# First token group's softmax and norms in halves of two tiles on three engines, second products of tiles 5 to 7 later, and unread matmuls in the waits

## The chip, the cores and the metric

One Trainium2 chip, one core of it. The metric is the device time of one execution of the whole kernel in microseconds; less is better. The kernel before took 384.93 us (median of 3 runs, 383.13 to 386.03).

## The reference, cut to what matters

Four blocks work on x of 4 x 256 tokens with 256 features. The first attention block fills most of the kernel and is the same in both kernels. The other three are where the change lies:

```python
def fp8_matmul(x2d, w):
    x8 = (x2d / scale_x).astype(float8_e4m3fn)
    w8 = (w / scale_w).astype(float8_e4m3fn)
    return (x8 @ w8.T) * (scale_x * scale_w)

x = x + L0_xattn(layernorm(x), ctx, ...)                        # x1
h = square(relu(fp8_matmul(layernorm(x), w_fc)))                # "expand"
x = x + fp8_matmul(h, w_proj)                                   # x2; "contract", the second products
scores = (qp @ kp.T) / 8 * layernorm(x)                         # qp, kp from ctx; gated by the normed x
x = x + softmax(where(mask, -inf, scores))                      # x3
y = layernorm(x)
h1 = rmsnorm(y, norm1_w);  h = y + (h1 @ wv + bv) @ wo          # "attend"
h2 = rmsnorm(h, norm2_w)
mlp = (silu(h2 @ w_gate) * (h2 @ w_up)) @ w_down                # 256 -> 704 -> 256
x = x + where(sigmoid(y @ w_router + b_router) > 0.5, h + mlp, y)
```

## The kernel before, in words

The 1024 tokens are 8 tiles of 128 rows (`NT`); a tile is one 128 x 256 slice of `xs` (the running x) and `xn` (its normed or gated form). Two groups of four tiles, 0 to 3 and 4 to 7, go one after the other through everything behind the expanding product. The matmuls of the last block run on 512 tokens, one group, at a time.

Each engine has its instruction list written out by hand, in the order in which it is issued; an engine works through its list in order, and a wait on a semaphore holds all that stands behind it. There is no planner: `@block.tensor`, `@block.vector`, `@block.scalar`, `@block.gpsimd` and `@block.sync` are the five lists, and semaphores (`x2_ready`, `norm_ready`, ...) tie them together. SyncE's list has only loads of weights, long done here, and the eight stores at the end.

For a group the steps are, with their engine and line:

- VectorE rounds `relu` (the squared activations) to two fp8 parts for each tile: `h8_halved(t)` (L1264) and `h8_shared(t)` (L1271). ScalarE turns the halved part into its form for the product, `rounded_top(t)` (L776). TensorE's `contract(t)` (L1832) multiplies both parts, 16 matmuls, and `x2_tile(t)` (L1183) on VectorE adds the result to `xs` and takes statistics.
- `aggregate` and `newton` give the inverse standard deviation. Its first guess is a power on GpSimd (`powers`, L535). Small steps that need each other have a semaphore wait between them (`in_order`).
- `gate_scores`, `mask_scores`, `largest` (L1195 to L1212) on VectorE make the masked scores of four tiles and their row maxima; `softmax(c)` (L791) on ScalarE is four Exp with row sums; `x3_sums` and `x3_statistics` (L1214, L1223) add the softmax to `xs` and take the statistics of the sum.
- `norm_rows(c)` (L802) on ScalarE normalises the four tiles. `turn_norm(c)` (L1843) on TensorE transposes them, `turned_copy` (L567) on ScalarE copies that to `tailT`, `attend(c)` (L1846) multiplies it with the folded value and output weights: 16 matmuls of 256 columns. GpSimd's `shifted_tiles` (L540) adds the bias row to the normed tiles.
- `h_tile(t)` (L1242) on VectorE makes h, `h_square_sum(t)` (L820) on ScalarE its sum of squares, `h_square` (L1249) and `newton` the scale, `h2_tiles` (L1255) the scaled rows. TensorE transposes them (`turn(2, atbuf, ...)`, L1872), `tail_copy` (L808) on ScalarE and `tail_lows` (L1316) on VectorE split them into a high and a low part.
- `gate_high(n)` and `gate_low(n)` (L1881, L1893) are gate and up for the n-th block of 128 of the 704 features. `silus(n)` (L830), `gated(n)` (L1333), `high_part(n)` (L837) and `low_part(n)` (L1340) make the activations, `down` (L1901) the last product.

In the order before, TensorE does the products of tiles 4 and 5 in one go ahead of the first group's transposes, and those of 6 and 7 right behind `attend(0)`. The second group's softmax chain starts when `x2_tile(7)` is done, so it lies beside the gate and up products of the first group. The Exp of all four tiles of the second group stand ahead of the first `silus`.

`keep_busy(n, spare, w)` (L1741) issues n bf16 matmuls of w columns (512 unless given) into a PSUM bank that nobody reads: they compute nothing of the result.

Of the kernel before, what the change touches and what calls it, by code (L numbers as in the profile page):

```python
# [23 lines left out]
P = 128  # L24
# [81 lines left out]
def build(nc, x, ctx_t, ctx_n, blob, const_a, const_b, wq1_t, wk1_t, attn_mask, key_mask,  # L106
          w_fc_t, w_proj_t, small, w_router, wv_t, wo, w_gate, w_up, w_down, out):
    with ExitStack() as ctx:
# [3 lines left out]
        def sem(name):  # L112
            return ctx.enter_context(nc.semaphore(name))
# [192 lines left out]
        v_first, shift3_ready = sem("v_first"), sem("shift3_ready")  # L306
        gated_high, gated_low = sem("gated_high"), sem("gated_low")
# [27 lines left out]
        def rots(n):  # L335

            return rot_low[n % 2][:], rot_up[:], rot_z[n % 2][:]

# [94 lines left out]
        def _(pool):  # L433
# [106 lines left out]
            def shifted_tiles(gr):  # L540

                pool.wait_ge(vo_copied, 3)
                for t in range(gr * NT // 2, (gr + 1) * NT // 2):
                    pool.wait_ge(norm_ready, NT + t + 1)
                    pool.tensor_tensor(atbuf(t), xn[:, t, :], bvo, ALU.add).then_inc(shifted_ready, 1)
# [12 lines left out]
            pool.wait_ge(norm_ready, 2 * NT)  # L558
# [7 lines left out]
        def _(act):  # L566
# [224 lines left out]
            def softmax(c):  # L791
                act.wait_ge(gated_ready, c + 1)
                for t in range(4 * c, 4 * c + 4):
                    act.activation(xn[:, t, :], xn[:, t, :], ACT.Exp, bias=c_m[:, t:t + 1],
                                   accum_out=ssq[:, t:t + 1]).then_inc(soft_ready, 1)
# [3 lines left out]
            softmax(0)  # L799
            rounded_top(5)  # L800

            def norm_rows(c):  # L802
                act.wait_ge(shift3_ready, c + 1)
                for t in range(4 * c, 4 * c + 4):
                    act.activation(xn[:, t, :], xs[:, t, :], ACT.Identity, bias=negmean[:, t:t + 1],
                                   scale=rstd[:, t:t + 1]).then_inc(norm_ready, 1)
# [11 lines left out]
            rounded_top(7)  # L818

            def h_square_sum(t):  # L820

                act.wait_ge(h_ready, t + 1)
                act.activation(mbias[:, t, :], hbuf(t), ACT.Square, accum_out=ssq[:, t:t + 1]).then_inc(ssq_ready, 1)

            for t in range(4):
                h_square_sum(t)
            tail_copy(0)
            softmax(1)
# [16 lines left out]
            silus(0)  # L845
            silus(1)
# [32 lines left out]
        def _(dve):  # L879
# [321 lines left out]
            def mask_scores(gr):  # L1201
                lo, hi = groups[gr]
                newton(4 + 4 * gr, rstd, lo, hi)
# [6 lines left out]
            def largest(gr):  # L1210
                lo, hi = groups[gr]
                dve.tensor_reduce(c_m[:, lo:hi], xn[:, lo:hi, :], AX, ALU.max, negate=True).then_inc(gated_ready, 1)  # L1212

            def x3_sums(gr):  # L1214

                lo, hi = groups[gr]
# [5 lines left out]

            def x3_statistics(gr):  # L1223

                lo, hi = groups[gr]
# [3 lines left out]
                in_order(ins)  # L1229
                aggregate(5 + 4 * gr, lo, hi)  # L1230
# [3 lines left out]

            def norm_tiles(gr):

                lo, hi = groups[gr]
                newton(5 + 4 * gr, rstd, lo, hi)
                for t in range(lo, hi):
                    normalise(t).then_inc(norm_ready, 1)  # L1240
# [36 lines left out]
            for t in range(3):  # L1277
# [12 lines left out]
            gate_scores(0)  # L1290
            mask_scores(0)
            largest(0)
            h8_shared(4)
            h8_halved(5)
            h8_shared(5)
            x3_sums(0)
            x3_statistics(0)
            x2_tile(4)
            newton(5, rstd, 0, half)
            dve.scalar_tensor_tensor(out=negmean[:, 0:half], in0=mv[:, 0:half, 0], scalar=-1.0, in1=rstd[:, 0:half],  # L1300
                                     op0=ALU.mult, op1=ALU.mult).then_inc(shift3_ready, 1)
            h8_halved(6)
            h8_shared(6)
            x2_tile(5)
            dve.wait_ge(variance_ready, 6)
            newton(6, r1, 0, half, of=(c_q, c_y1))
            h8_halved(7)
            h8_shared(7)
            for t in range(half):
                h_tile(t)  # L1310
            h_square(0)
            x2_tile(6)
            dve.wait_ge(variance_ready, 7)
            newton(7, r2, 0, half)
            h2_tiles(0)
            def tail_lows(c):  # L1316
# [6 lines left out]

            in_order(x2_tile(7))
# [3 lines left out]
            mask_scores(1)  # L1328
            largest(1)
            tail_lows(0)  # L1330
            x3_sums(1)

# [42 lines left out]
            x3_statistics(1)  # L1375
# [54 lines left out]
        def _(pe):  # L1430
# [412 lines left out]
            def turn_norm(c):  # L1843
                turn(1, lambda t: xn[:, t, :], norm_ready, NT, (2 * c, 2 * c + 1))
# [15 lines left out]
            keep_busy(18, 1)  # L1860
            contract(4)
            contract(5)
            keep_busy(16, 1)
            pe.wait_ge(qk_copied, 8)
            turn_norm(0)
            attend(0)
            contract(6)
            contract(7)

            pe.wait_ge(wgu_low, 4)  # L1870
            keep_busy(10, 4)
# [47 lines left out]
            pe.wait_ge(h_ready, 4)  # L1919
            pe.wait_ge(x2_ready, NT)  # L1920
            for n in range(3):
                gate_high(n)
# [102 lines left out]
```

## Time and profile before

| | before |
|---|---|
| median of 3 runs | 384.93 us (383.13 to 386.03) |
| the profiled execution's time | 386.52 us |
| its span, first to last instruction | 384.4 us |
| mean granted TensorE clock | 0.991 |
| TensorE busy | 366.5 us (95%) |
| VectorE busy | 295.8 us (77%) |
| ScalarE busy | 208.5 us (54%) |
| GpSimd busy | 174.5 us (45%) |

The span is what the trace covers; the profiled execution's time holds 2.1 us more around it. The granted clock is the share of full TensorE speed that the chip granted (1.00 is 2.4 GHz, 0.50 is 1.2 GHz). Busy shares are means over stages with different limits. The changed part begins near 294 us and ends near 346 us; all ahead of it is the same in both kernels, and all behind it is the same work in the same order. A start time in the rows below is counted from the first instruction; "idle before" with a releaser names what the engine waited for.

### The profile page before, as it was taken

Reading aid. Unit: us, or ns where it says so; the run is one execution under the profiler, and the core shown is the slowest. Engines: PE = TensorE matmul, PEld = TensorE weight load, DVE = VectorE, ACT = ScalarE, POOL = GpSimd, SP = SyncE. Lnnn points to the kernel's source line nnn. Section 1 sums busy time; section 2 is a strip of 40 time slices with the busy share of each in tenths; the row PEclk is TensorE's granted clock in tenths of the full one; section 3 lists DMA queues with packets and bytes.
Section 4 is the critical chain, followed back from the end, with each engine's and each line's share of the span. In section 5 each row is a group of like instructions: output and inputs, shape, how many; then the busy total and the mean of one; then the engine's idle time right before and its main releaser. Section 6 shows DMA issues by size and latency. Waiting matters only on the chain.

```text
span 384.4 us, 6374 instructions
## 1 busy us (share of the span) xinstructions
PE 366.5 (95%) x2185; PEld 267.3 (70%) x2185; DVE 295.8 (77%) x674; ACT 208.5 (54%) x555; POOL 174.5 (45%) x163
## 2 busy tenths in 40 slices
PE   8799999999999999999999999998999789989996
PEld 8775676677676766776767677764556467879885
DVE  5698698698667886976697765578899967897773
ACT  1524476457546664765576494617974362582240
POOL 2454665476448645764665430671801232056100
PEclk9999999999999999999999999999999969999999
DMA  7639100300301103000004000400000000000001
GB/s 245 213 112 342 62 1 0 111 3 1 112 0 46 65 0 112 3 0 2 0 3 150 3 0 2 119 0 3 0 3 0 0 2 0 3 0 2 28 28 56
DMA packets 9087, 17.55 MB, mean 46 GB/s; under 512 B 2144, under 2 KB 6944, under 8 KB 8160
## 3 DMA queue, kind: packets, MB, share of 16 engines
q1 hardware_dynamic: 9056, 17.14, 13.3%
q8 instruction: 18, 0.29, 0.3%
q14 instruction: 13, 0.11, 0.1%
HBM read 16.09 MB, written 1.05 MB: 45 GB/s over the span
## 4 chain that ended last, share of the span: by engine, by line
PE 67%; DVE 14%; ACT 7%; POOL 6%; issue 3%; DMA 2%; SPq 0%; DVEq 0%; POOLq 0%
PE bank L1524 16%; PE bank L1595 7%; PE bank L1570 7%; PE bank L1586 6%; PE bank L1554 4%; PE bank L1539 3%; PE bank L1476 3%; PE bank L1616 2%; PE bank L1839 2%; DVE relu L1159 2%; PE bank L1443 2%; DMA blobs<-in_blob 2%; POOL prob L463 2%; PE bank L1851 2%; PE bank L1445 1%
## 5 line engine op out<-in xcount | busy, mean ns | idle before, releaser
L463 POOL TENSOR_TENSOR prob<-prob,rinv 128x512 f32<-128x512 f32 x64 | 65.9, 1041 | 74.4 <-DVE rinv L1023 74.4
L1524 PE MATMUL bank<-xnT,w 128*128 128x512 f32 x288 | 90.2, 434 | 1.7 <-DVE xnT L920 1.7
L621 ACT ACTIVATE prob<-bank,negmax 128x256 f32<-128x256 f32 x128 | 59.0, 478 | 29.5 <-DVE negmax L1017 29.5
L1017 DVE TENSOR_REDUCE negmax<-bank 128x2 f32<-128x512 f32 x64 | 40.8, 680 | 35.3 <-PE bank L1570 35.3
L1524 PEld LDWEIGHTS bank<-xnT,w 128*128 128x128 f32 x288 | 50.4, 189 | 19.5 <-issue 13.3
L631 ACT COPY probT<-bank 128x512 f32<-128x512 f32 x64 | 37.7, 589 | 22.8 <-PE bank L1586 22.8
L951 DVE TENSOR_TENSOR rot_up<-bank,cb 64x512 f32<-64x512 f32 x64 | 44.1, 689 | 1.6
L458 POOL TENSOR_TENSOR rot_low<-rot_low,rot_up 128x512 f32<-128x512 f32 x32 | 41.0, 1281 | 3.8 <-DVE rot_up L951 3.8
L1586 PE MATMUL bank<-ca,prob 128*128 128x128 f32 x256 | 39.4, 276 | 0.5 <-ACT probT L631 0.3
L1586 PEld LDWEIGHTS bank<-ca,prob 128*128 128x128 f32 x256 | 29.1, 140 | 13.8 <-issue 5.3
L443 POOL TENSOR_TENSOR c_y<-c_ve,minus_half 128x4 f32<-128x4 f32 (+1 forms) x9 | 9.8, 1086 | 61.2 <-DVE c_ve L901 45.5
L1570 PEld LDWEIGHTS bank<-ktmp,uT 64*128 64x128 f32 x256 | 23.4, 186 | 13.4 <-issue 11.3
L1570 PE MATMUL bank<-ktmp,uT 64*128 64x256 f32 x256 | 32.0, 389 | 0.0
L456 POOL TENSOR_TENSOR rot_z<-rot_z 128x512 f32<-128x512 f32 x16 | 21.1, 1322 | 23.8 <-DVE rot_z L951 23.8
L1595 PE MATMUL bank<-probT,kva 128*64 128x256 f32 x256 | 31.1, 384 | 0.5
L1616 PE MATMUL bank<-wkvo,cT 128*128 128x256 f32 x128 | 29.7, 381 | 0.0
L621 ACT ACTIVATION_READ_ACCUMULATOR prob<-bank,negmax 128x1 f32 x128 | 26.7, 209 | 0.0
L1595 PEld LDWEIGHTS bank<-probT,kva 128*64 128x64 f32 x256 | 17.7, 137 | 12.7 <-ACT probT L631 3.9
L1616 PEld LDWEIGHTS bank<-wkvo,cT 128*128 128x128 f32 x128 | 23.5, 190 | 3.9 <-issue 1.2
L946 DVE TENSOR_TENSOR rot_low<-bank,cb 128x512 f32<-128x512 f32 x32 | 21.9, 685 | 4.6 <-PE bank L1524 4.6
L636 ACT COPY cT<-bank 128x512 f32<-128x512 f32 x15 | 8.8, 585 | 28.4 <-PE bank L1595 28.4
L951 DVE TENSOR_TENSOR rot_z<-bank,cb 64x512 f32<-64x512 f32 x32 | 22.0, 688 | 0.4
(212 smaller groups left out, 706.8 us busy)
## 6 DMA issues: line engine op xcount, KB each, us to landing
blobs<-in_blob SPq DMA_DIRECT2D x7, 1024.0 KB, 4.9
xs<-in_x SPq DMA_DIRECT2D x2, 512.0 KB, 4.1
xn<-in_w_fc_t SPq DMA_DIRECT2D x1, 1024.0 KB, 4.9
ctxT<-in_w_proj_t SPq DMA_DIRECT2D x1, 1024.0 KB, 5.3
out<-qk SPq DMA_DIRECT2D x8, 128.0 KB, 1.7
cb<-in_const_b SPq DMA_DIRECT2D x1, 768.0 KB, 9.0
blobs<-in_w_gate SPq DMA_DIRECT2D x1, 704.0 KB, 5.2
blobs<-in_w_up SPq DMA_DIRECT2D x1, 704.0 KB, 6.5
```

Of the source, the lines that this page charges most:

```text
L458: pool.tensor_tensor(low[:, r, :], low[:, r, :], up[:, r, :], ALU.add).then_inc(joined, 1)
L463: pool.tensor_tensor(p[:], p[:], rinv[:, n % PROBS, :].unsqueeze(2).to_broadcast([P, 2, S]), ALU.mult).then_inc(normed, 1)
L621: ins = act.activation(prob[n % PROBS][:, st, :], pS[n % UNITS][:, st * S:(st + 1) * S], ACT.Exp, bias=negmax[:, n % UNITS, st:st + 1], ac ...
L631: act.copy(probT[n % UNITS][:].rearrange("p a s -> p (a s)"), pT[:]).then_inc(probsT_copied, 1)
L946: dve.tensor_tensor(tokens(rope_parts(m)[0]), tokens(src[:]), angles(cosq, r), ALU.mult)
L951: ins = dve.tensor_tensor(tokens(crossed[to:to + DC, :]), tokens(src[lo:lo + DC, :]), angles(sinq, r, lo, lo + DC), ALU.mult)
L1017: dve.tensor_reduce(negmax[:, n % UNITS, :], pS[n % UNITS][:].rearrange("p (a s) -> p a s", a=2), AX, ALU.max, negate=True).then_inc(max_r ...
L1524: ins = pe.matmul(q_bank(m)[:], w[a][:, k, r * P:(r + 1) * P], x[b][:, k, c * CH:(c + 1) * CH], start=(i == 0), stop=(i == 5))
L1570: ins = pe.matmul(pS[2 * a + h][:, st * S:(st + 1) * S], uT[g % 2][lo:hi, at:at + P], ktmp[lo:hi, b * S:(b + 1) * S], start=True, stop=True)
L1586: ins = pe.transpose(pT[:, lt * S + st * P:lt * S + (st + 1) * P], prob[n % PROBS][:, st, lt * P:(lt + 1) * P], ident)
L1595: ins = pe.matmul(o[h * DC:(h + 1) * DC, :], kva[:, 2 * b + lt, :], probT[2 * a + h][:, lt, :], start=(lt == 0), stop=(lt == 1))
L1616: return pe.matmul(bank[OUT_BANK[t // 2]][:, t % 2 * D:(t % 2 + 1) * D], cT[:, f, t * P:(t + 1) * P], wkvo[:, f, :], start=(f == 0 and t % ...
```

## The change

It moves and splits work; no product, softmax or norm is dropped. `normalise(t)` is an existing helper (L904), one VectorE `tensor_scalar` for a tile.

1. The first group's (and the second's) `mask_scores`, `largest`, `softmax` and `x3_sums` now take two tiles at a time, `two` = 0 to 3. The statistics stand in `x3_sums`; `x3_squares` holds what is left of `x3_statistics`.
2. In the first group tiles 0 and 1 are normalised on VectorE, tiles 2 and 3 on ScalarE; a new semaphore `first_normed` counts the former, and `norm_of(t)` says what to wait for.
3. The h8 roundings of tiles 5 to 7 and `x2_tile` of 4 to 6 stand at other places of VectorE's list, `rounded_top(7)` behind `h_square_sum`.
4. TensorE: `contract(5)` behind `attend(0)`, `contract(7)` behind `gate_high(0)`. Unread matmuls: 25 for 18, 19 for 16 at another place, 4 new ones ahead of `attend(0)`, and 10 taken out ahead of the transposes of h2.
5. ScalarE runs `softmax(2)`, `silus(0)`, `softmax(3)`, `silus(1)`, where it ran one softmax of four tiles ahead of the first `silus`.

The diff, cut to its core:

```diff
+        def norm_of(t):
+            return (first_normed, t + 1) if t < 2 else (norm_ready, NT + t - 1)
...
 # GpSimd: shifted_tiles
-                    pool.wait_ge(norm_ready, NT + t + 1)
+                    pool.wait_ge(*norm_of(t))
...
 # ScalarE
-            def softmax(c):
-                act.wait_ge(gated_ready, c + 1)
-                for t in range(4 * c, 4 * c + 4):
+            def softmax(two):
+                act.wait_ge(gated_ready, two + 1)
+                for t in range(2 * two, 2 * two + 2):
...
             softmax(0)
+            softmax(1)
             rounded_top(5)
             def norm_rows(c):
                 act.wait_ge(shift3_ready, c + 1)
-                for t in range(4 * c, 4 * c + 4):
+                for t in range(2 if c == 0 else 4, 4 * c + 4):
...
             norm_rows(0)
             turned_copy(4, tailT, turned_copied, (0, 1))
             rounded_top(6)
-            rounded_top(7)
             for t in range(4):
                 h_square_sum(t)
+            rounded_top(7)
             tail_copy(0)
-            softmax(1)
+            softmax(2)
...
             silus(0)
+            softmax(3)
             silus(1)
...
 # VectorE
             gate_scores(0)
+            newton(4, rstd, 0, half)
             mask_scores(0)
             largest(0)
+            mask_scores(1)
+            largest(1)
             h8_shared(4)
+            x3_sums(0)
+            in_order(x3_sums(1))
+            aggregate(5, 0, half)
             h8_halved(5)
-            h8_shared(5)
-            x3_sums(0)
-            x3_statistics(0)
-            x2_tile(4)
             newton(5, rstd, 0, half)
             dve.scalar_tensor_tensor(out=negmean[:, 0:half], ...).then_inc(shift3_ready, 1)
+            for t in range(2):
+                normalise(t).then_inc(first_normed, 1)
+            x3_squares(0)
+            h8_shared(5)
             h8_halved(6)
-            h8_shared(6)
-            x2_tile(5)
             dve.wait_ge(variance_ready, 6)
             newton(6, r1, 0, half, of=(c_q, c_y1))
+            h_tile(0)
+            x2_tile(4)
+            h_tile(1)
+            h_tile(2)
+            h_tile(3)
+            h8_shared(6)
+            h_square(0)
             h8_halved(7)
             h8_shared(7)
-            for t in range(half):
-                h_tile(t)
-            h_square(0)
-            x2_tile(6)
             dve.wait_ge(variance_ready, 7)
             newton(7, r2, 0, half)
             h2_tiles(0)
+            x2_tile(5)
...
+            tail_lows(0)
+            x2_tile(6)
             in_order(x2_tile(7))
             aggregate(8, half, NT)
             dve.wait_ge(qk_copied, 8)
             gate_scores(1)
-            mask_scores(1)
-            largest(1)
-            tail_lows(0)
-            x3_sums(1)
+            newton(8, rstd, half, NT)
+            mask_scores(2)
+            largest(2)
+            mask_scores(3)
+            largest(3)
+            x3_sums(2)
...
             gated(0)
-            x3_statistics(1)
+            in_order(x3_sums(3))
+            aggregate(9, half, NT)
+            x3_squares(1)
             gated(1)
...
 # TensorE
             pe.wait_ge(x2_ready, 3)
-            keep_busy(18, 1)
+            keep_busy(25, 1)
             contract(4)
-            contract(5)
-            keep_busy(16, 1)
+            keep_busy(19, 1)
             pe.wait_ge(qk_copied, 8)
             turn_norm(0)
+            keep_busy(4, 1)
             attend(0)
+            contract(5)
             contract(6)
-            contract(7)
             pe.wait_ge(wgu_low, 4)
-            keep_busy(10, 4)
             turn(2, atbuf, h2_ready, 0, (0, 1))
...
             pe.wait_ge(h_ready, 4)
+            gate_high(0)
+            contract(7)
+            gate_high(1)
             pe.wait_ge(x2_ready, NT)
-            for n in range(3):
-                gate_high(n)
+            gate_high(2)
             for n in range(3):
                 gate_low(n)
```

## Rows read from the trace of the kernel before

**Rows 1.** Timeline of TensorE, first group: start us, length us, work, idle before.
```profile
300.08 3.65 PE L1839 MATMUL bank<-wpr,tail_all 128*128 128x256 bf16 x32 [1.66 <-DVE tail_all L1273]
303.57 3.62 PE L1743 MATMUL bank<-wfc,ident 128*128 128x512 bf16 x16
308.13 0.73 PE L1438 MATMUL bank<-ca,xn 128*128 128x128 f32 x2 [0.94 <-ACT xn L805]
...
311.00 6.78 PE L1851 MATMUL bank<-cb,tailT 128*128 128x256 f32 x16 [0.72 <-ACT tailT L571]
317.62 3.66 PE L1839 MATMUL bank<-wpr,tail_all 128*128 128x256 bf16 x32
...
324.74 0.47 PE L1890 MATMUL bank<-tail_hi,wgu_high 128*128 128x512 f32 x1 [0.43 <-ACT tail_hi L812]
```

**Rows 2.** Windows view: stretch, length, busy of each engine, granted clock, DMA.
```profile
310.40:311.00 0.60, 0.00 (x0) 0.00 (x0) 0.56 (x2) 0.60 (x3) 0.60 (x2) 0.50 0.00 0
```

**Rows 3.** The timeline of TensorE, second group.
```profile
339.87 1.03 PE L1438 MATMUL bank<-ca,xn 128*128 128x128 f32 x8
341.72 3.69 PE L1851 MATMUL bank<-cb,tailT 128*128 128x256 f32 x16 [0.82 <-ACT tailT L571]
345.60 0.39 PE L1443 MATMUL bank<-wd_high,gated_hi 128*128 128x256 f32 x1 [0.18 <-DVE h_rows L1246]
```

**Rows 4.** The timeline of VectorE from 298 us on.
```profile
298.06 1.22 DVE L1212 TENSOR_REDUCE c_m<-xn 128x4 f32<-128x1024 f32 x1
299.19 0.74 DVE L1273 TENSOR_SCALAR tail_all<-relu,sc 128x1024 fp8e4<-128x1024 f32 x1
...
301.63 1.67 DVE L1220 SCALAR_TENSOR_TENSOR xs<-xn,c_r,xs 128x256 f32<-128x256 f32 x4
...
305.07 0.17 DVE L901 TENSOR_SCALAR c_ve<-mv 128x4 f32<-128x4 f32 x1
...
309.45 0.52 DVE L891 SCALAR_TENSOR_TENSOR c_t<-c_y 128x4 f32<-128x4 f32 x1
...
317.82 0.48 DVE L1246 SCALAR_TENSOR_TENSOR h_rows<-bank,r,at_rows 128x256 f32<-128x256 f32 x1 [0.80 <-PE bank L1851]
318.88 0.17 DVE L1252 TENSOR_SCALAR c_ve<-ssq 128x4 f32<-128x4 f32 x1 [0.58 <-ACT mbias L823]
...
321.00 1.14 DVE L1260 TENSOR_SCALAR at_rows<-h_rows,r 128x256 f32<-128x256 f32 x4
322.06 0.48 DVE L1186 SCALAR_TENSOR_TENSOR xs<-bank,sc,xs 128x256 f32<-128x256 f32 x1
...
335.99 0.68 DVE L1337 TENSOR_TENSOR tail_all<-bank,tail_all 128x512 f32<-128x512 f32 x1
...
338.22 1.29 DVE L1337 TENSOR_TENSOR tail_all<-bank,tail_all 128x512 f32<-128x512 f32 x2
```

**Rows 5.** The timeline of ScalarE.
```profile
301.30 1.04 ACT L779 ACTIVATE tail_all<-prob 128x1024 bf16<-128x1024 fp8e4 x1
307.38 2.08 ACT L805 ACTIVATE xn<-xs,negmean,rstd 128x256 f32<-128x256 f32 x4 [5.05 <-DVE negmean L1300]
...
323.91 1.26 ACT L812 ACTIVATE tail_hi<-bank,sm 128x512 fp32r<-128x512 f32 x2 [5.06 <-PE bank L1438]
...
330.31 0.50 ACT L794 ACTIVATE xn<-xn,c_m 128x256 f32<-128x256 f32 x1
...
330.92 1.28 ACT L835 ACT_TABLE_LOAD   x1
332.21 1.09 ACT L835 ACTIVATE tail_all<-bank 128x512 f32<-128x512 f32 x2
```

**Rows 6.** The page's costliest groups: a reduction of 512 columns.
```profile
L1017 DVE TENSOR_REDUCE negmax<-bank 128x2 f32<-128x512 f32 x64 | 40.8, 680 | 35.3 <-PE bank L1570 35.3
```

**Rows 7.** The timeline of GpSimd.
```profile
308.12 3.18 POOL L545 TENSOR_TENSOR at_rows<-xn,cb 128x256 f32<-128x256 f32 x4 [0.82 <-ACT xn L805]
...
336.52 1.01 POOL L443 TENSOR_TENSOR c_y<-c_q,minus_half 128x4 f32<-128x4 f32 x1
```

More of the change, by code:

```diff
@@ L306, in build @@
         v_first, shift3_ready = sem("v_first"), sem("shift3_ready")
+        first_normed = sem("first_normed")
         gated_high, gated_low = sem("gated_high"), sem("gated_low")
@@ L556, in _ @@
             powers(11, 1, c_ve, c_y)
-            pool.wait_ge(norm_ready, 2 * NT)
+            pool.wait_ge(*norm_of(NT - 1))
             pool.wait_ge(h2_ready, NT)
@@ L1199, in gate_scores, with mask_scores @@
                                              op0=ALU.subtract, op1=ALU.mult).then_inc(gate_done, 1)
-            def mask_scores(gr):
-                lo, hi = groups[gr]
-                newton(4 + 4 * gr, rstd, lo, hi)
+            def mask_scores(two):
+                lo, hi = 2 * two, 2 * two + 2
                 dve.wait_ge(gate_done, hi)
@@ L1208, in mask_scores, with largest, x3_sums @@
                 in_order(ins)
-            def largest(gr):
-                lo, hi = groups[gr]
+            def largest(two):
+                lo, hi = 2 * two, 2 * two + 2
                 dve.tensor_reduce(c_m[:, lo:hi], xn[:, lo:hi, :], AX, ALU.max, negate=True).then_inc(gated_ready, 1)
-            def x3_sums(gr):
-                lo, hi = groups[gr]
+            def x3_sums(two):
+                lo, hi = 2 * two, 2 * two + 2
                 dve.wait_ge(soft_ready, hi)
@@ L1221, in x3_sums @@
                                              in1=xs[:, t, :], op0=ALU.mult, op1=ALU.add).then_inc(x3_ready, 1)
-            def x3_statistics(gr):
-                lo, hi = groups[gr]
                 for t in range(lo, hi):
@@ L1228, in x3_statistics, with x3_squares @@
                     ins = dve.bn_stats(stats[:, t, :], xs[:, t, :])
-                in_order(ins)
-                aggregate(5 + 4 * gr, lo, hi)
+                return ins
+            def x3_squares(gr):
+                lo, hi = groups[gr]
                 in_order(dve.reciprocal(c_q[:, lo:hi], c_ve[:, lo:hi]))
@@ L1233, in x3_statistics @@
                 dve.tensor_scalar(c_q[:, lo:hi], c_q[:, lo:hi], 1e-6, None, ALU.add).then_inc(variance_ready, 1)
[L1235 to L1240, printed above, removed]
             def h_tile(t):
@@ L1843, in turn_norm @@
             def turn_norm(c):
-                turn(1, lambda t: xn[:, t, :], norm_ready, NT, (2 * c, 2 * c + 1))
+                for k in range(DK):
+                    for t in range(4):
+                        if k == 0:
+                            pe.wait_ge(*norm_of(4 * c + t))
+                        ins = pe.transpose(bank[4 + 2 * c + k][:, t * P:(t + 1) * P],
+                                           xn[:, 4 * c + t, k * P:(k + 1) * P], ident)
+                    ins.then_inc(turned, 1)
             def attend(c):
```

## The prediction

> **What bounds the kernel now.** I read the granted clock first, then TensorE's rows in time order, then the chain of waits and the rows of VectorE, ScalarE and GpSimd around it. TensorE is busy 95% of the span, so I looked for where its start times come from. Between the products of tile 3 and `gate_high(0)` (L1921) it mostly runs matmuls that nobody reads. It waits for `h8_shared(4)`, then for the normalised rows; transposes run from 308.13 us, `attend(0)` from 311.00 [rows 1]. The granted clock is 0.50 there, the 1.2 GHz level [rows 2]. The 16 matmuls of `attend(0)` take 6.78 us; the same 16 in `attend(1)` take 3.69 at the full clock [rows 1, 3]. So the profiled execution holds a clock loss of 3.09 us in front of everything later. Its time was 386.52 us (span 384.4 and 2.1 around it); without that loss it would be 383.4, near the lowest of the three runs, 383.13. The median, 384.93, lies 1.6 below the profiled execution, and I take the spread for that loss in different lengths.
>
> From 324.74 to 339.87 TensorE runs 66 matmuls of gate and up without a gap, 0.229 us each [rows 1, 3]: `gate_high` (8 of them) is 1.83, `gate_low` (4) 0.92. What sets the end lies beside it: `x2_tile(7)` at 322.06, statistics, gating, softmax of tiles 4 to 7, the Silu table at 330.92, `gated`, `norm_rows(1)`, `gated(2)` at 338.22, and the products `down_two(0)` at 345.60, released by VectorE's `h_tile(5)` [rows 3, 4, 5]. The reader is to see two queues with nearly the same end: TensorE is free for transposes at 339.87, and the last rows they need come at 339.8. So the change pays only as far as it moves `x2_tile(7)` and `gated(2)`.
>
> **The change, first group.** (a) *Softmax in halves.* The reduction of 1024 columns takes 1.22 us; for 512 I take 0.69, between half of it (0.61) and the 0.68 of a 128x512 reduction elsewhere [rows 4, 6]. Two reductions and one more wait put the last maximum at 299.51 instead of 299.28, but ScalarE has tiles 0 and 1 done by 299.1 and starts the last two at 299.54. A tile costs it 0.50 [rows 5], so the exponentials end at 300.6 (301.4 before). VectorE has `h8_shared(4)` done at 300.17 (0.66 a step, 0.74 long) [rows 4] and goes straight into the sums: `h8_halved(5)` and `h8_shared(5)`, 1.32 us, no longer stand ahead. Sums, statistics and aggregates of four tiles took 3.44 (301.63 to 305.07) [rows 4]; with one more reciprocal, 0.2, `c_ve` starts at 304.01, 1.06 earlier.
>
> (b) *Norms on three engines.* The power on GpSimd takes 1.01 [rows 7] and ends at 305.27; `h8_halved(5)` (to 304.94) lies beside it, and `rounded_top(5)`, 1.04 on ScalarE [rows 5], ends at 306.03, just ahead of `norm_rows`. The Newton steps and the shift end at 306.04. VectorE normalises tiles 0 and 1 (0.28 a step, as `h2_tiles`) [rows 4], ScalarE tiles 2 and 3 at 0.52 each [rows 5]: last row at 307.16, before 309.46. The transposes, copies and `attend` followed the last row by 1.54 (309.46 to 311.00), so `attend(0)` starts at 308.7, 2.3 earlier. The unread matmuls cost nothing while they end inside waits: 0.217 each [rows 1], 25 of them end at 299.8 before `contract(4)` (300.25 to 302.0), 19 end at 306.15, and the 4 behind the transposes 0.1 before `attend`. If they overran, the bounds are nothing and 0.9 us, all four. I take nothing. With them no stretch without matmuls is longer than 0.4 us, so I expect 3.7 us for `attend(0)`: end 312.4.
>
> (c) *h and h2.* `x3_squares(0)`, after the two norms, gives GpSimd its second power until 308.2; `shifted_tiles(0)` runs to 311.4. `newton(6)` lies beside it and was slow there, 1.9 us (309.45 to 311.33, first step 0.52) [rows 4]; bounds 0.6 and 1.9, and I take 1.9: VectorE is free for `h_tile(0)` at 310.3. `x2_tile(4)` (0.9) goes behind it; `h_tile(3)` waits for `attend`: 312.5, before 317.82. The row sum, power, Newton steps and `h2_tiles` take 1.06, 1.25, 0.7 and 1.14 [rows 4, 7]: h2 is ready at 316.67; `h8_shared(6)`, `h8_halved(7)` and `h8_shared(7)` fit into the waits, `rounded_top(7)` (314.4 to 315.5) too. ScalarE copies 0.45 after the last row, and `gate_high(0)` follows the copy's start by 0.83 (323.91 to 324.74) [rows 1, 5]: 317.95, 6.8 earlier than before.
>
> (d) *Later products.* A `contract` is 1.75 (two took 3.66) [rows 1]. 5 and 6 run 312.45 to 315.95, beside the wait for h2, at no cost; were that cover gone they would cost 3.5. `contract(7)` comes behind `gate_high(0)`: 319.8 to 321.55, and `x2_tile(7)` at 321.7. **Before it was 322.06, so of 6.8 us only 0.36 reach the second group.** `x2_tile(5)`, the two `tail_lows` and `x2_tile(6)` end at 320.0, so none delays it.
>
> **The change, second group.** From `x2_tile(7)` to the maxima as before, minus 0.36; halves give the first maximum at 327.11, the last at 328.65. ScalarE now runs `softmax(2)`, `silus(0)`, `softmax(3)`, `silus(1)`. Before, the only table load between Exp and Silu took 1.28, from 330.92, and Silu began at its end, 332.21 [rows 5]. With Exp again behind Silu there are three loads instead of one, 2.57 us more. Exp ends for tiles 4 and 5 at 328.15; load, `silus(0)` to 330.05; load to 331.34; Exp of tiles 6 and 7 to 332.35 (all four before: 330.9); load, `silus(1)` to 334.25. VectorE has the sums of tiles 4 and 5 done and `gated(0)` at 330.93. Behind 332.38 stand 0.21 + 0.84 + 0.7 for tiles 6 and 7, aggregates 0.6: `c_ve` done at 334.74, GpSimd's two powers to 336.85, Newton steps 0.6, `gated(2)` at 337.45, before 338.22. **Gain 0.77**: halving saves more on this chain than the two loads take. What is queued behind is `norm_rows(1)`, 337.05 instead of 337.72, then the same copies, `low_part`s beside GpSimd's shifts, `h_tile(5)`, and `down_two(0)` at 344.8 for 345.60. `gate_high(4)` waits for `gated(0)` (331.0) and `gate_high(5)` for `gated(1)`, at 335.99 before and 335.95 now [rows 4]: TensorE stands idle from 333.7 to 336.0, time it had won. From 345.60 on both kernels do the same work, so the 0.77 stays.
>
> The Trainium skill, "ScalarE: Activation LUTs", section "What ACT_TABLE_LOAD costs", gives about 1.28 us for the load and about 1.38 more for a drain at every switch; its section "Table sets: the hidden batching unit" asks for all calls of one set together, which speaks against this order. By its price, two switches instead of none before the last Exp would give 388.5 us by my estimate. The row here has no drain behind the load.
>
> Sum: 386.52 - 0.77 = **385.7 us**, 0.8 above the median of the runs before, 0.8 below the profiled one, and 2.3 above 383.4, what the old order takes when its clock holds. It is no measurable change. Within 1% means 381.1 to 388.8; less than 1% is about what a measurement of this kernel can't tell from nothing.
>
> **The rivals.** *The clock falls in the second wait (slower).* Place: TensorE between 333.7 and 340.65. In it lie 2.3 us idle, six matmuls (1.4 us), 0.8 idle, eight transposes, 0.75 idle; before the loss at 310.4 stood 3.8 us with only eight transposes [rows 1, 2]. It decides if the clock is down when `attend(1)` starts at 340.65: at 6.78 it would end at 347.4, and `down_two(0)` waits for it and not for `h_tile(5)`: 2.6 us later, 388.3, slower than before by 1.8 against the profiled execution and 3.4 against the median; with the products behind it slow too, up to 390. Against: the idle 1.66 us before 300.08 [rows 1] and the 0.82 before `attend(1)` [rows 3] did not lower it, and the six matmuls break the stretch. 0.22. *A switch costs more than its row*, or the first half's close fits (`rounded_top(5)`, the 4 unread matmuls) fail: each 0.1 to 2.7, to 388.4. 0.06. *Silu and Exp share one table.* Then Exp of tiles 6 and 7 ends at 331.0 and `gated(2)` comes at 336.1: 384.4. Against: a load stands between Exp and Silu now. 0.06. *TensorE is the bound after all*: the six gate steps, 15.13, and `contract(7)` from 317.95 end at 334.9, 4.9 before 339.87: 381.6, down to 380 if the second group follows. It needs my chain from `x2_tile(7)` to `gated(2)` to be 4 us too long, though it is made of rows. 0.10.
>
> **How the numbers follow.** Forecast 0.56, with its own range of 384.2 to 387.2: newton(6) at 0.6 takes nothing off, since `h_tile(3)` waits for TensorE; a reduction of 0.61 takes 0.3 off; the run-to-run spread is 383.1 to 386.0. The range 382.8 to 388.3 leaves out most of the last rival and the upper half of the first. Faster by over 1%: 0.6 of the last rival and a tail of the forecast, 0.10. Slower by over 1%: the first rival's upper part, 0.09, and the second's, 0.03: 0.12. Within 1%: 0.78.
>
> **What would show it.** Right: granted clock 1.00 at the first `attend` and 3.7 us for it; `gate_high(0)` near 318; `x2_tile(7)` within 0.5 of 321.7; four ACT_TABLE_LOADs in all instead of two; an idle TensorE in front of `gate_high(5)`; `gated(2)` near 337.5. Wrong: no load around `softmax(3)`; `x2_tile(7)` before 320; a clock of 0.50 in `attend(1)`; `down_two(0)` more than 1 us from 344.8.

## The result

| | before | after |
|---|---|---|
| median, 22 runs each | 385.24 us (382.92 to 387.51) | 386.51 us (385.40 to 388.56) |
| ratio to before | | 1.0042, 95% interval 1.0024 to 1.0061 |
| profiled execution, its span | 386.52, 384.4 us | 387.64, 385.9 us |
| mean granted clock in it | 0.991 | 0.987 |
| TensorE, VectorE, ScalarE, GpSimd busy | 366.5, 295.8, 208.5, 174.5 us | 368.6, 296.9, 210.5, 175.0 us |

The change makes no difference above 1%; it is slower by 0.42%, 1.3 us between the medians. The forecast was 385.7, 0.8 above the median known then. The ratios here and below leave out executions of the kernel before that took over 1.5% more than its fastest (none here, five of the 35 beside the first four experiments), so a ratio need not be the quotient of two medians.

**Three stretches.** Between the first `gate_scores` and `down_two(0)` lies all that the change touches. I cut it at two starts of VectorE that every kernel of this study has: `gate_scores(1)`, right behind `x2_tile(7)` and its statistics, and `gated(2)`. The numbers are differences of start times in each kernel's timeline.

| kernel | `gate_scores(0)` to `gate_scores(1)` | to `gated(2)` | to `down_two(0)` | sum |
|---|---|---|---|---|
| before | 29.50 | 14.57 | 7.38 | 51.45 |
| after, as predicted | 29.14 | 14.16 | 7.35 | 50.65 |
| after | 29.97 | 14.42 | 7.34 | 51.73 |

In the profiled execution of before the first stretch holds the clock loss of 3.09 us [rows 1, 2]. Without it the sum would be 48.4, and the kernel before with only its unread matmuls changed, below, has 48.41. Against that the change is 3.3 us slower from here to there.

### The profile page after: what moved, and what is told of

The parts are those of the page before. It is cut to its first block, busy times and chain, and to the rows that moved or that the text cites. A ratio compares the mean times of both kernels' runs of the same rounds, so it can differ in the third digit from the quotient of the medians.

```text
span 385.9 us, 6385 instructions
## 1 busy us (share of the span) xinstructions
PE 368.6 (96%) x2184; PEld 266.6 (69%) x2189; DVE 296.9 (77%) x680; ACT 210.5 (55%) x555; POOL 175.0 (45%) x163
## 4 chain that ended last, share of the span: by engine, by line
PE 73%; DVE 13%; ACT 6%; POOL 3%; issue 2%; DMA 2%; SPq 0%; DVEq 0%; POOLq 0%
PE bank L1536 16%; PE bank L1607 8%; PE bank L1582 8%; PE bank L1598 7%; PE bank L1628 6%; PE bank L1566 4%; PE bank L1551 3%; PE bank L1488 3%; PE bank L1851 2%; DVE relu L1166 2%; PE bank L1455 2%; DMA blobs<-in_blob 2%; PE bank L1908 2%; PE bank L1909 2%; POOL c_y L448 2%
```

## The profile after

TensorE, first group: start, length, engine, line, instructions, idle before.

```profile
295.79 5.34 PE L1755 MATMUL bank<-wfc,ident 128*128 128x512 bf16 x24 [0.16 <-issue]
301.47 1.91 PE L1851 MATMUL bank<-wpr,tail_all 128*128 128x256 bf16 x16 [0.34 <-DVE tail_all L1271]
303.22 4.26 PE L1755 MATMUL bank<-wfc,ident 128*128 128x512 bf16 x18
307.59 1.47 PE L1861 MATMUL bank<-ca,xn 128*128 128x128 f32 x8
308.90 1.03 PE L1755 MATMUL bank<-wfc,ident 128*128 128x512 bf16 x4
309.79 3.72 PE L1870 MATMUL bank<-cb,tailT 128*128 128x256 f32 x16
313.35 3.76 PE L1851 MATMUL bank<-wpr,tail_all 128*128 128x256 bf16 x32
317.89 1.46 PE L1450 MATMUL bank<-ca,at_rows 128*128 128x128 f32 x8 [0.78 <-DVE at_rows L1258]
319.78 0.47 PE L1908 MATMUL bank<-tail_hi,wgu_high 128*128 128x512 f32 x1 [0.43 <-ACT tail_hi L818]
...
321.76 1.92 PE L1851 MATMUL bank<-wpr,tail_all 128*128 128x256 bf16 x16
```

Against [rows 1]: the wait of 1.66 us ahead of `contract(4)` is 0.34, unread matmuls fill up to 307.5 and again behind the transposes, and `attend(0)` takes 3.72 us for 6.78. Subtract 1.20 us for comparison with [rows 1 to 7]: `gate_scores(0)` starts at 295.35 here and at 294.15 there. That offset comes from ahead of the change, where this execution has a stretch at half clock that the profiled execution of before had not. The windows view, with columns stretch, length, busy time (instructions), granted clock, DMA:

```profile
261.00:267.00 6.00, 6.00 (x14) 0.50 0.00 0
339.40:342.30 2.90, 2.70 (x11) 0.50 0.00 0
```

The second of these lies in the changed part: the clock fell behind an idle 2.27 us ahead of `gate_high(5)`, and was up again for `attend(1)`. TensorE there, first the wait, then the transposes of the second group, `attend(1)` and `down_two(0)`:

```profile
338.24 0.50 PE L1908 MATMUL bank<-tail_hi,wgu_high 128*128 128x512 f32 x1 [2.27 <-DVE tail_all L1347]
```

```profile
340.48 2.19 PE L1861 MATMUL bank<-ca,xn 128*128 128x128 f32 x8 [0.20 <-DVE tail_all L1347]
343.44 3.69 PE L1870 MATMUL bank<-cb,tailT 128*128 128x256 f32 x16 [0.77 <-ACT tailT L576]
347.08 0.39 PE L1455 MATMUL bank<-wd_high,gated_hi 128*128 128x256 f32 x1
```

Against [rows 3] the eight transposes take 2.19 us for 1.03, but `attend(1)` takes the same 3.69. VectorE, the terms of the prediction in order of time:

```profile
299.98 0.69 DVE L1218 TENSOR_REDUCE c_m<-xn 128x2 f32<-128x512 f32 x1
...
305.07 0.17 DVE L908 TENSOR_SCALAR c_ve<-mv 128x4 f32<-128x4 f32 x1
...
309.87 0.61 DVE L898 SCALAR_TENSOR_TENSOR c_t<-c_y 128x4 f32<-128x4 f32 x1 [0.30 <-POOL c_y L448]
...
313.15 1.25 DVE L1244 SCALAR_TENSOR_TENSOR h_rows<-bank,r,at_rows 128x256 f32<-128x256 f32 x3
...
314.99 0.17 DVE L1250 TENSOR_SCALAR c_ve<-ssq 128x4 f32<-128x4 f32 x1
...
317.39 1.14 DVE L1258 TENSOR_SCALAR at_rows<-h_rows,r 128x256 f32<-128x256 f32 x4
...
323.72 0.48 DVE L1193 SCALAR_TENSOR_TENSOR xs<-bank,sc,xs 128x256 f32<-128x256 f32 x1 [1.79 <-PE bank L1851]
...
332.21 0.69 DVE L1347 TENSOR_TENSOR tail_all<-bank,tail_all 128x512 f32<-128x512 f32 x1
334.62 0.17 DVE L1224 RECIPROCAL c_r<-ssq 128x2 f32<-128x2 f32 x1 [1.72 <-ACT xn L799]
...
339.74 1.29 DVE L1347 TENSOR_TENSOR tail_all<-bank,tail_all 128x512 f32<-128x512 f32 x2
```

The reader is to see the second reduction to maxima at 299.98, the first `c_ve` of x3 at 305.07, the slow Newton step beside GpSimd (0.61), three `h_tile` in one row without a wait (313.15), h2 at 317.39, `x2_tile(7)` behind 1.79 us of waiting for `contract(7)`, `gated(0)`, the wait for the last Exp ahead of the sums of tiles 6 and 7, and `gated(2)`. ScalarE between, with three loads where [rows 5] has one:

```profile
330.28 1.28 ACT L841 ACT_TABLE_LOAD   x1
331.58 0.60 ACT L841 ACTIVATE tail_all<-bank 128x512 f32<-128x512 f32 x1
332.19 1.28 ACT L799 ACT_TABLE_LOAD   x1
333.49 0.51 ACT L799 ACTIVATE xn<-xn,c_m 128x256 f32<-128x256 f32 x1
...
334.60 1.28 ACT L841 ACT_TABLE_LOAD   x1
335.90 0.60 ACT L841 ACTIVATE tail_all<-bank 128x512 f32<-128x512 f32 x1
```

GpSimd's powers of four columns in the first group. The second and the third have two h8 roundings each beside them on VectorE and take 1.44 and 1.45 us; the first has `h8_halved(5)` alone beside it (305.27 to 306.05) and takes 1.01, as the power in [rows 7]:

```profile
305.32 1.01 POOL L448 TENSOR_TENSOR c_y<-c_ve,minus_half 128x4 f32<-128x4 f32 x1 [8.91 <-DVE c_ve L908]
308.33 1.44 POOL L448 TENSOR_TENSOR c_y<-c_q,minus_half 128x4 f32<-128x4 f32 x1 [2.00 <-DVE c_q L1238]
...
315.24 1.45 POOL L448 TENSOR_TENSOR c_y<-c_ve,minus_half 128x4 f32<-128x4 f32 x1 [2.71 <-DVE c_ve L1250]
```

## The experiments

All times are medians. The kernel before was timed beside each group: 385.26 us for the first four experiments, 385.01 for the next four, 384.81 for the last two. The changed kernel's 386.51 is from yet another group, with 385.24, so a difference from it of 0.4 us or less says nothing by itself; the stretches, from the profiled executions, are the finer measure. "Stretches" are those of the table above.

**One load, ScalarE's list alone.** Edit to the changed kernel:

```diff
+            softmax(3)
             silus(0)
-            softmax(3)
             silus(1)
```

> The changed kernel with softmax(3) moved ahead of silus(0) on ScalarE alone, so one table load instead of three behind the first Exp; VectorE's order stays (gated(0) ahead of the sums of tiles 6 and 7). Theory (the chain from x2_tile(7) to gated(2) sets the end, and its queue on VectorE decides): the two loads go, 2.57 us, but silus(0) now ends near 333.6 in the time of the changed kernel's trace, gated(0) near 334.3, and it stands ahead of x3_sums(3), which began at 334.62: so only about 0.4 us comes back, some 386.1 where the changed kernel has 386.5. Rival (the loads cost their full price wherever they stand): 2.6 us come back, 383.9. Second rival (the loads are hidden anyway): nothing.

Measured 386.13 us, as expected; ratio to before 1.0015 (0.9983 to 1.0048). Stretches 30.00, 14.12, 7.35. Two loads less give 0.30 us of the second stretch, not 2.57: VectorE waits for `silus(0)` instead, with the sums of tiles 6 and 7 queued behind `gated(0)`:

```profile
332.50 0.69 DVE L1347 TENSOR_TENSOR tail_all<-bank,tail_all 128x512 f32<-128x512 f32 x1 [1.42 <-ACT tail_all L841]
```

**One load, both lists.**

```diff
+            in_order(x3_sums(3))
             gated(0)
-            in_order(x3_sums(3))
             aggregate(9, half, NT)
```

> As the one before, and on VectorE the sums of tiles 6 and 7 stand ahead of gated(0). Theory: x3_sums(3) starts at the end of x3_sums(2), near 332.2 instead of 334.6, gated(0) adds 0.6 behind it, so c_ve and gated(2) come 1.8 us earlier, and the kernel takes about 384.7. TensorE waits for gated(0) until 334.6 ahead of gate_high(4), 1.6 us longer, at no cost. Rival (TensorE's gate products are the bound): that later gated(0) makes it 1.5 us slower than the changed kernel, 388.

Measured 384.92 us; 1.0004 (0.9971 to 1.0037). Stretches 29.99, 12.59, 7.88. The second stretch is 1.83 shorter, as expected; 0.54 of it is lost in the third. I had put TensorE's longer wait for `gated(0)` at no cost. Behind that wait of 1.94 us the granted clock was 0.50 from 335 to 337 us, and TensorE came to the transposes at 339.27, though the last normed row was there at 338.19:

```profile
333.43 0.50 PE L1908 MATMUL bank<-tail_hi,wgu_high 128*128 128x512 f32 x1 [1.94 <-DVE tail_all L1347]
```

The loads cost what they delay on VectorE's queue, 1.8 us up to `gated(2)`, and the order of both engines has to change to get it back.

**Tile 7 early.** `contract(7)` ahead of the transposes of h2, its bank 3 instead of 7:

```diff
-MLP_BANK = (6, 7, 1, 3, 6, 7, 6, 7)
+MLP_BANK = (6, 7, 1, 3, 6, 7, 6, 3)
...
-                if t >= 4:
+                if t == 7:
+                    pe.wait_ge(h_ready, 4)
+                elif t >= 4:
...
             contract(6)
+            contract(7)
...
             gate_high(0)
-            contract(7)
-            gate_high(1)
             pe.wait_ge(x2_ready, NT)
+            gate_high(1)
             gate_high(2)
...
-            tail_lows(0)
             x2_tile(6)
             in_order(x2_tile(7))
...
             largest(3)
+            tail_lows(0)
             x3_sums(2)
```

> The changed kernel with contract(7) back ahead of the transposes of h2, in a bank that is free by then, so that it does not wait for x2_tile(5); x2_tile(5), (6), (7) stand in one row on VectorE, tail_lows(0) behind the last maximum. Halves and three loads stay. Theory: x2_tile(7) comes near 320.1 in the time of the changed kernel's trace instead of 323.72, 3.6 us earlier, the transposes of h2 about 0.9 later, and TensorE waits 2 us for tail_lows(0); the chain carries 3.6 us to the end: 382.9. Rival (TensorE is the bound once the first group is late again): no more than 1.5 us, 385.0 or above.

Measured 384.88 us; 1.0014 (0.9984 to 1.0044): 1.6 us below the changed kernel, not 3.6. Stretches 26.40, 15.86, 8.23. The first stretch gives the 3.57 that were expected. The second gives 1.44 back, and the third 0.89. TensorE had to wait for `tail_lows(0)` ahead of `gate_low(0)`, and ScalarE for `gate_low(0)` ahead of `silus(0)`, with `softmax(3)` queued behind it:

```profile
324.75 1.28 ACT L841 ACT_TABLE_LOAD   x1
327.48 0.60 ACT L841 ACTIVATE tail_all<-bank 128x512 f32<-128x512 f32 x1 [1.45 <-PE bank L1919]
```

TensorE in the same kernel: the wait for `tail_lows(0)`, and `attend(1)` partly at the half clock (0.50 from 340 to 342 us), 5.38 us for 3.69, which holds up `down_two(0)`.

```profile
325.82 0.50 PE L1919 MATMUL bank<-tail_lo,wgu_high 128*128 128x512 f32 x1 [1.84 <-DVE tail_lo L1326]
...
338.86 5.38 PE L1872 MATMUL bank<-cb,tailT 128*128 128x256 f32 x16 [0.82 <-ACT tailT L576]
```

My theory named the chain rightly and missed two things on it. The rival's number is the nearer one, though the chain, not the transposes of h2, spent the difference. It is also a case in which a clock loss in the second group costs time, as the first rival of the prediction had it.

**Tile 7 early and one load.** The edits of the second and third kernels.

> The third and the second kernel together. Theory: the sum of both would be 5.4 us, but the gate products, pushed behind tail_lows(0), then end near 337.9 and the normed rows near 336.5, so TensorE becomes the bound again: 4 to 4.5 us, 382.0 to 382.5. Rival (everything on the chain adds up): 381.1.

Measured 383.64 us; 0.9970 (0.9941 to 0.9999). Stretches 26.39, 13.91, 9.05. It is 1.1 us above the theory's 382.0 to 382.5, further from the rival's 381.1. `gated(2)` is done at 333.95, but TensorE comes to the transposes only at 337.77: it waited 1.81 us for `tail_lows(0)`, and ran the `gate_low`s behind it slowly, 11 matmuls in 4.27 us, with a granted clock of 0.50 from 329 to 331 us.

```profile
326.07 0.49 PE L1919 MATMUL bank<-tail_lo,wgu_high 128*128 128x512 f32 x1 [1.81 <-DVE tail_lo L1326]
326.73 4.27 PE L1919 MATMUL bank<-tail_lo,wgu_high 128*128 128x512 f32 x11 [0.16 <-DVE tail_lo L1326]
...
337.77 1.03 PE L1863 MATMUL bank<-ca,xn 128*128 128x128 f32 x8
```

**Lows first.** The kernel before this one with `tail_lows(0)` at another place:

```diff
             in_order(x2_tile(7))
             aggregate(8, half, NT)
+            tail_lows(0)
...
             largest(3)
-            tail_lows(0)
             x3_sums(2)
```

> Tile 7 early and one load, with tail_lows(0) right behind the aggregates of tile 7 instead of behind the last maximum. In the run with them behind it, TensorE waited 1.8 us for tail_lows(0), its clock fell in the gate products behind that wait (11 of them took 4.27 us instead of 2.79), and gated(2) had been done 3.8 us before TensorE came to the transposes. Theory (TensorE is the bound there): this takes the wait and the slow stretch away, costs the chain 1.3 us that it has to spare, and gives 382.0. Rival (VectorE's chain is the bound): 1.3 us slower than 383.6, 384.9.

Measured **381.92 us** (7 executions), as expected; 0.9923 (0.9886 to 0.9960), 0.8% faster than before, and faster than the changed kernel. Stretches 27.71, 12.55, 7.37; `tail_lows(0)` now stands ahead of `gate_scores(1)`, so its 1.3 us count in the first of them and no longer in the second. The wait and the slow stretch are gone, and the second group's transposes come 2.8 us and `attend(1)` 2.5 us earlier, counted from `gate_scores(0)`, than in the kernel before this one:

```profile
307.99 3.72 PE L1872 MATMUL bank<-cb,tailT 128*128 128x256 f32 x16
...
324.00 2.88 PE L1919 MATMUL bank<-tail_lo,wgu_high 128*128 128x512 f32 x12
...
337.01 3.69 PE L1872 MATMUL bank<-cb,tailT 128*128 128x256 f32 x16 [0.82 <-ACT tailT L576]
341.18 0.39 PE L1455 MATMUL bank<-wd_high,gated_hi 128*128 128x256 f32 x1 [0.48 <-DVE h_rows L1244]
```

**Unread matmuls in the kernel before.**

```diff
             contract(5)
-            keep_busy(16, 1)
+            keep_busy(20, 1)
             pe.wait_ge(qk_copied, 8)
             turn_norm(0)
+            keep_busy(4, 1)
             attend(0)
```

> The kernel before with unread matmuls alone changed: 20 instead of 16 ahead of the first group's transposes, and 4 more between the transposes and attend(0), as the changed kernel has them. Theory: the stretch of 3.8 us with only eight transposes no longer lets the clock fall, attend(0) takes 3.7 us in every run, and since the chain to the end hangs on it, the median falls to the runs of before in which the clock held: 383.4 to 384.0 instead of 385.2. Rival (the spread of before has another source, the clock at attend(0) is off the path): 385.2.

Measured 383.38 us; 0.9956 (0.9929 to 0.9982). Stretches 26.46, 14.58, 7.37: the first is 3.04 shorter than in the profiled execution of before. `attend(0)`:

```profile
311.87 3.72 PE L1851 MATMUL bank<-cb,tailT 128*128 128x256 f32 x16
```

Nine of its 12 executions had a mean clock of 1.000 and took 382.6 to 383.5 us. The kernel before, timed beside it, spread from 382.34 to 387.92, this one from 382.64 to 385.15. So a good part of the spread of before is this clock loss, and eight more matmuls that nobody reads give 1.6 us.

**No unread matmuls in the changed kernel.**

```diff
             contract(4)
-            keep_busy(19, 1)
             pe.wait_ge(qk_copied, 8)
             turn_norm(0)
-            keep_busy(4, 1)
             attend(0)
```

> The changed kernel without the 19 and the 4 unread matmuls around the first group's transposes. Theory: TensorE has only eight transposes between 303.2 and 309.8 us of the changed kernel's trace, the granted clock is 0.50 in attend(0), which takes 6.7 us instead of 3.72, and all of it reaches x2_tile(7) and the end: 386.5 + 3.0 = 389.5. Rival (the first group's gain was off the path anyway, so its loss is too): 386.5 to 387.

Measured 389.41 us (6 executions); 1.0102 (1.0063 to 1.0142), as expected. Stretches 32.50, 14.41, 7.35: `attend(0)` at the half clock, and its delay goes through to `x2_tile(7)`.

```profile
309.47 6.36 PE L1870 MATMUL bank<-cb,tailT 128*128 128x256 f32 x16 [0.68 <-ACT tailT L576]
```

**The second group whole.**

```diff
             mask_scores(2)
-            largest(2)
             mask_scores(3)
-            largest(3)
-            x3_sums(2)
+            dve.tensor_reduce(c_m[:, half:NT], xn[:, half:NT, :], AX, ALU.max, negate=True).then_inc(gated_ready, 2)
+            dve.wait_ge(soft_ready, NT)
+            in_order(dve.reciprocal(c_r[:, half:NT], ssq[:, half:NT]))
+            for t in range(half, NT):
+                dve.scalar_tensor_tensor(out=xs[:, t, :], in0=xn[:, t, :], scalar=c_r[:, t:t + 1],
+                                         in1=xs[:, t, :], op0=ALU.mult, op1=ALU.add).then_inc(x3_ready, 1)
...
             gated(0)
-            in_order(x3_sums(3))
+            for t in range(half, NT):
+                dve.wait_ge(x3_ready, t + 1)
+                ins = dve.bn_stats(stats[:, t, :], xs[:, t, :])
+            in_order(ins)
             aggregate(9, half, NT)
...
+            softmax(3)
             silus(0)
-            softmax(3)
             silus(1)
```

> The changed kernel with the second group's maxima, sums and statistics over four tiles at once and softmax(2) and softmax(3) ahead of silus(0), as before: neither halves nor extra loads in the second group. Theory: what halving gains there (about 1.8 to 2 us by the run with one load on both engines, which came 1.6 below the changed kernel) and what the two extra loads cost cancel, so gated(2) follows x2_tile(7) by 16.2 us, as in the kernel before, where the changed kernel has 16.0: 386.6. Rival (the loads are the whole cause of the change's failure): 384.5 or less.

Measured 386.62 us; 1.0042 (1.0018 to 1.0066), as expected. Stretches 29.98, 14.75, 7.35. Halves with three loads take 14.42, halves with one load 12.59, four tiles at once with one load 14.75: up to `gated(2)`, halving the second group is worth 2.2 us, and its order on ScalarE and VectorE cost 1.8 of them. Up to `down_two(0)` it is 1.6 and 1.3, since the kernel with one load on both lists loses 0.54 there.

**The power by itself.** `h8_halved(7)` and `h8_shared(7)` behind the Newton steps:

```diff
             h_square(0)
-            h8_halved(7)
-            h8_shared(7)
             dve.wait_ge(variance_ready, 7)
             newton(7, r2, 0, half)
+            h8_halved(7)
+            h8_shared(7)
             h2_tiles(0)
```

> The changed kernel with h8_halved(7) and h8_shared(7) behind the Newton steps of the second norm instead of ahead of them, so that they no longer run beside GpSimd's power of four columns. Theory (those VectorE instructions slow GpSimd): the power at 315.24 us of the changed kernel's trace takes 1.0 us again instead of 1.45, as the one in the kernel before with no such instruction beside it; the rows of h2 come about 0.9 us later in all, since 1.3 us of rounding now stands ahead of them, and the kernel takes 387.4. Rival (the longer power has another cause): 1.45 again, and 1.3 us later.

Measured 386.94 us for the 387.4 expected; 1.0054 (1.0022 to 1.0086). The power for h2 takes 1.02 us here; the one ahead of it, which still has two roundings beside it, stays at 1.44:

```profile
306.44 1.44 POOL L448 TENSOR_TENSOR c_y<-c_q,minus_half 128x4 f32<-128x4 f32 x1 [2.00 <-DVE c_q L1238]
...
313.35 1.02 POOL L448 TENSOR_TENSOR c_y<-c_ve,minus_half 128x4 f32<-128x4 f32 x1 [2.71 <-DVE c_ve L1250]
```

So the slower power comes from the two roundings beside it. Whether one of them alone does it, `h8_shared` say, is not shown: `h8_halved(5)` beside the power at 305.32 us of the changed kernel did nothing to it. The time is no clean measure of the delay: in the profiled execution the longer wait of TensorE ahead of the transposes of h2 is followed by a granted clock of 0.50 from 319 to 322 us, in `gate_high(0)`, and the first stretch is 32.38, 2.4 longer than in the changed kernel where the delay of h2 accounts for 0.9. The transposes behind that wait, and a microsecond of `gate_high(0)` in the windows view:

```profile
316.89 1.46 PE L1450 MATMUL bank<-ca,at_rows 128*128 128x128 f32 x8 [1.67 <-DVE at_rows L1258]
```

```profile
320.00:321.00 1.00, 1.00 (x4) 0.50 0.00 0
```

**Norms on ScalarE.**

```diff
-            return (first_normed, t + 1) if t < 2 else (norm_ready, NT + t - 1)
+            return (norm_ready, NT + t + 1)
...
-                for t in range(2 if c == 0 else 4, 4 * c + 4):
+                for t in range(4 * c, 4 * c + 4):
...
-            for t in range(2):
-                normalise(t).then_inc(first_normed, 1)
             x3_squares(0)
```

> The changed kernel with all four norms of the first group on ScalarE again. Theory: the last normed row comes 1.0 us later (four rows of 0.52 instead of two), so do attend(0), h2, gate_high(0) and x2_tile(7), and that reaches the end: 387.5. Rival (the first group is off the path): 386.5.

Measured 386.60 us; 1.0046 (1.0018 to 1.0074). Stretches 30.59, 14.41, 7.35. By its median this is the rival's number: the kernel is not told from the changed one. Its profiled execution shows the delay all the same. `attend(0)` starts 15.42 us behind `gate_scores(0)` (293.55 in this kernel) instead of 14.44, the 1.0 us that was expected, but the last `h_tile` ends only 0.6 later:

```profile
308.97 3.72 PE L1868 MATMUL bank<-cb,tailT 128*128 128x256 f32 x16
```

```profile
312.73 0.48 DVE L1244 SCALAR_TENSOR_TENSOR h_rows<-bank,r,at_rows 128x256 f32<-128x256 f32 x1 [0.38 <-PE bank L1868]
```

Here VectorE waits 0.38 us for `attend`; in the changed kernel it did not wait, since its own queue was the later one. 0.6 of the 1.0 us reaches the second group in the profiled execution (first stretch 30.59 for 29.97).

## Why the prediction was right

The result, 386.5 us, lies in the range, and the difference from before is below 1%, as forecast. Not all of the mechanism held. The changed part was to be 0.80 us shorter than in the profiled execution of before, and is 0.28 longer (51.73 for 51.45). Of the marks that the prediction set for being right, `x2_tile(7)` is 0.82 from 321.7 where 0.5 was allowed, and `gated(2)` came at 338.54 for 337.5. `down_two(0)`, at 345.88, is 1.08 from 344.8, which the prediction had named as a mark of being wrong. The number stands because the missed 1.08 us are small against a range of 382.8 to 388.3. By its steps:

- **Softmax in halves, norms on three engines: right.** Less the offset of 1.20, `c_ve` starts at 303.87 (304.01 predicted) and `attend(0)` at 308.59 (308.7). The three close fits held: `rounded_top(5)`, the 19 and the 4 unread matmuls, and the clock stayed up; the kernels that add or drop those matmuls show what they hold, 2.5 to 3.0 us in the first stretch. What this step is worth for the second group is another matter. With tile 7 early the first stretch is 26.40, and it is 26.46 in before's order with the clock up: the halves and the shared norms moved the second group's start by 0.06 us, though `attend(0)` starts 2.4 us earlier. VectorE is busy for 24.50 of those 26.40 us, so its queue, more than `attend(0)`, sets that point.
- **h and h2: 0.66 too early.** The rows of h2 began at 316.19 where 315.53 was predicted. I had `h_tile(3)` wait for `attend(0)`, at 312.5. It started near 312.7, behind the other tiles: VectorE's queue decided, with `newton(6)` slow beside GpSimd and `x2_tile(4)` put between; the norms on ScalarE alone show it. The failed term is the cost of the roundings that I had "fit into the waits" at nothing. GpSimd's power for h2 took 1.45 instead of 1.01 with two of them beside it, which the power by itself shows. The power ahead of `newton(6)` took 1.44, also with two beside it, and `h_tile(0)` started at 310.69 where 310.3 was predicted; that these 0.4 us come from the roundings too was not tested.
- **Later products: right in kind, 0.8 off.** `gate_high(0)` at 318.58 (317.95), `contract(7)` behind it, `x2_tile(7)` at 322.52 (321.7): nothing of more than 6 us reaches the second group; where I had a gain of 0.36 us it lost 0.47. 0.63 of the 0.8 is h2 above, and the first eight gate products took 1.98 us (319.78 to 321.76) where I had 1.83, the mean of all 66. The kernel with `contract(7)` early moves that point by 3.6 us. So the place of `contract(7)`, with what follows from it on VectorE's queue, is what makes the change slower than before's order with the clock up: the first stretch is 29.97 for 26.46 there, and the second group gives back 0.2 of these 3.5 us.
- **The second group's loads: right in cause, 0.26 off in size.** Four loads in all; 14.42 us for 14.16 predicted. I had halving save a little more than the loads take. The kernel with the second group whole has 14.75 for that stretch and 386.62 us for the whole: 0.3 more by the stretch, no difference by the median. The Trainium skill, "ScalarE: Activation LUTs", section "Table sets: the hidden batching unit", wants calls of one set together. The trace agrees: the two more changes between Exp and Silu brought two more loads of 1.28 us. The 1.38 us drain at each switch, from its section "What ACT_TABLE_LOAD costs", is not in the rows here: 330.28 + 1.28 is 331.56, and the Silu starts at 331.58.
- **TensorE idle ahead of `gate_high(5)`: right,** 2.27 us for 2.3.
- **The rivals.** The clock did fall in the second wait of the profiled execution, at 339.4, but was back before `attend(1)`, so it cost nothing there (7.34 us in the last stretch, 7.38 before); clock losses in the second group came with 0.9 us more in that stretch with tile 7 early, and 0.5 with one load on both lists. TensorE as the bound was wrong for this kernel, and became right once the chain was shortened. One table for Silu and Exp, and switches dearer than their row, were wrong.
- **The comparison.** I held the sum against one execution with a full clock loss. In all ten profiled executions that have the four unread matmuls ahead of it `attend(0)` takes 3.72 us, and the changed kernel still is slower. At a mean clock of 1.000 before's order takes 382.6 to 383.5 us (by the kernel with unread matmuls alone changed) and the one such run of the changed kernel 386.0, 2.5 to 3.4 more, where the prediction gave 2.3. That is one run only, and five of the changed kernel's with a mean clock of 0.996 are faster, 385.4 to 385.7; but the fastest run of each, 382.64 and 385.40, are 2.8 apart as well. My remark that TensorE "mostly runs matmuls that nobody reads" in the first group was wrong, though nothing hangs on it: from 294.36 us to `gate_high(0)` at 324.74 they take 10.0 us (4.06, 3.62 and 2.32).

What stays open: what the clock losses ahead of the changed part, such as the one at 261 us, depend on, and how much of the 1.3 us between the medians each clock loss makes. That the h8 roundings of tile 7 could run behind h2 altogether was not tried: their input shares its memory with `tail_hi`, which `tail_copy(0)` writes next.

## What to carry to other kernels

A transfer of work between groups pays by how far it moves the start of the chain that sets the end, not by how much earlier the other engine begins: read the first instruction of that chain (`x2_tile(7)` here) and what is put ahead of it on each queue. Here `contract(7)` behind `gate_high(0)` took away 3.6 us. Where two functions of different table sets alternate on ScalarE, count the loads, and look for who is queued behind them on the engine that consumes; changing ScalarE's list alone gave 0.3 of 1.8 us. And before a restructuring is compared, look whether the spread of the old kernel is a clock loss: eight unread matmuls in its wait gave 1.6 us by themselves, and the changed kernel with the moves that the traces pointed to (tile 7 early, one load, lows first) is 1.5 below that.

## What the runs showed of the hardware

- A power of four columns on GpSimd takes 1.01 to 1.02 us alone and 1.44 to 1.45 with two of VectorE's fp8 roundings of 1024 columns beside it, `h8_shared` and `h8_halved`, in every kernel where they meet; with `h8_halved(5)` alone beside it, it took 1.01. VectorE's Newton steps of four columns take 0.51 to 0.65 beside GpSimd's additions of a tile, 0.14 to 0.17 elsewhere.
- A table load does not wait for the semaphore of the activation behind it: in the kernel with tile 7 early it runs at 324.75, and the Silu starts 1.45 us after its end, at 327.48.
- The same wait of 2.27 us ahead of `gate_high(5)` was followed by the half clock in the profiled execution of the changed kernel and by the full one in that of the kernel with the norms on ScalarE. The clock fell behind 1.67 us in the kernel with the power by itself, and held behind 1.66 us in the kernel before.
